# Rotary swap by bank, held-back weight splits and new instruction orders in a two-layer attention and LoRA-expert kernel on one core

## The reference

```python
x = x + attn(layernorm(x), w_qkv, w_o)            # causal, 32 query heads, 8 key heads, head size 16, rotary
x = x + ffn(layernorm(x))                         # base matmul + bias + two of eight LoRA experts, gated
x = x + attn(layernorm(x), [wq, wk, wv], wo)      # second set of attention weights
x = x + ffn(layernorm(x))                         # the same ffn weights
# x: (8, 256, 512) float32
def attn(x, w, w_o):
    q, k, v = split(x @ w)                        # 512 + 128 + 128 columns
    q, k = rope(q), rope(k)                       # pairs of neighbouring rows: (x1 c - x2 s, x1 s + x2 c)
    p = softmax(mask(q k^T / 4)); return (p v) @ w_o
def ffn(x):
    g = softmax(top2(x @ gate_w.T))
    return x @ base_w.T + base_b + 2 * sum_e g_e (x @ A_e.T) @ B_e.T
```

## Time and profile before

| what | us |
|---|---|
| median of 3 runs (lowest, highest) | 797.63 (794.98, 800.29) |
| profiled execution | 798.41 |
| span of its trace, first to last instruction | 796.6 |

### The profile page before, as it was taken

How to read it: one execution, slowest core, us unless ns; L and a number is a source line. 1 busy time by engine, 2 the same in 40 slices (tenths; PEclk the granted TensorE clock), 3 DMA queues, 4 the chain that set the end, 5 groups by cost and what they waited for, 6 DMA issues and landing times.

```text
span 796.6 us, 15039 instructions
## 1 busy us (share of the span) xinstructions
PE 741.6 (93%) x4340; PEld 558.2 (70%) x4340; DVE 564.2 (71%) x2769; ACT 492.4 (62%) x1086; POOL 567.7 (71%) x671
## 2 busy tenths in 40 slices
PE   7599889999999999799999999999999999999975
PEld 6575458777777777577777787777777768664654
DVE  5766759597586869658695968778696856877423
ACT  7425556666676756656676776767666576665522
POOL 4645784969587886968689895969778497955512
PEclk9787999999999999999999999999999999999989
DMA  8442434442434444444445635253444425342010
GB/s 316 134 118 63 121 74 114 122 105 100 106 111 128 119 129 113 141 103 116 126 119 143 158 100 122 96 125 108 117 113 126 116 68 130 104 102 76 25 49 28
DMA packets 47835, 89.30 MB, mean 112 GB/s; under 512 B 15364, under 2 KB 18180, under 8 KB 47752
## 3 DMA queue, kind: packets, MB, share of 16 engines
q1 hardware_dynamic: 45448, 87.29, 40.3%
q10 hardware_dynamic: 2304, 1.05, 0.5%
HBM read 24.34 MB, written 9.44 MB: 42 GB/s over the span
## 4 chain that ended last, share of the span: by engine, by line
PE 69%; DVE 8%; DMA 7%; POOL 6%; ACT 5%; issue 4%; SPq 1%; POOLq 0%; ACTq 0%; DVEq 0%
PE T L440 10%; PE SB L424 9%; PE SA L403 5%; PE T L382 5%; PE T L383 4%; PE T L384 4%; DVE SA L949 4%; PE SA L407 4%; PE T L452 3%; PE T L453 3%; PE T L454 3%; PE T L476 3%; DMA QK<-mT 3%; PE T L477 3%; PE T L478 3%
## 5 line engine op out<-in xcount | busy, mean ns | idle before, releaser
L949 DVE CUSTOM_DVE_ANT_0 SA<-SA,mask 128x128 f32<-128x128 f32 (+1 forms) x1024 | 332.6, 385 | 62.6 <-PE SA L407 32.4
L745 ACT ACTIVATE PT<-SB 128x512 f32<-128x512 f32 x384 | 216.2, 596 | 67.0 <-PE SB L424 56.9
L1104 POOL TENSOR_SCALAR_AFFINE_SELECT PT<-PT 128x512 f32<-128x512 f32 x256 | 159.2, 634 | 95.1 <-ACT PT L745 94.6
L424 PE MATMUL SB<-QK 100*128 100x512 f32 x384 | 149.1, 427 | 11.7 <-ACT PT L745 8.1
L949 DVE DVE_READ_ACCUMULATOR2_ANT nm<- 128x1 f32 x1024 | 140.7, 137 | 0.1
L382 PE MATMUL T<-XH,WQh 128*128 128x256 f32 x384 | 113.5, 296 | 7.6 <-DVE XL L915 6.2
L403 PE MATMUL SA<-QK 96*128 96x512 f32 x256 | 105.7, 428 | 5.9 <-DVE nm L949 5.4
L383 PE MATMUL T<-XL,WQh 128*128 128x256 f32 x384 | 110.6, 288 | 0.0
L384 PE MATMUL T<-XH,WQl 128*128 128x256 f32 x384 | 110.4, 287 | 0.0
L424 PEld LDWEIGHTS SB<-QK 100*128 100x128 f32 x384 | 71.0, 192 | 40.8 <-ACT PT L745 22.1
L440 PE MATMUL T<-PT,V 128*32 128x512 f32 x768 | 92.7, 617 | 1.3 <-POOL PT L1104 1.3
(11 more groups left out here) (102 smaller groups left out, 1641.7 us busy)
## 6 DMA issues: line engine op xcount, KB each, us to landing
QK<-Rh SPq DMA_DIRECT2D x64, 256.0 KB, 4.0
QK<-R SPq DMA_DIRECT2D x64, 192.0 KB, 3.7
Qs<-Qf SPq DMA_DIRECT2D x32, 320.0 KB, 2.9
QK<-R SPq DMA_DIRECT2D x64, 128.0 KB, 3.7
ND<-sums SPq DMA_DIRECT2D x64, 128.0 KB
ND<-EF SPq DMA_DIRECT2D x32, 128.0 KB, 2.0
mid<-X SPq DMA_DIRECT2D x16, 256.0 KB, 2.7
X<-mid SPq DMA_DIRECT2D x8, 512.0 KB, 4.1
```

Source lines behind the costliest of these rows:

```text
L424: e.matmul(SB[k % 2][:, :].rearrange("p (j q) -> p j q", j=4), keys(p, 100)[:, u % 2, i // 2, :], queries(p, 100)[:, :, min(i, 1), :], sta ...
L745: e.activation(PT[:, k % RING, :], SB[k % 2][:, :], ACT.Exp, scale=0.25).then_inc(S["ex"], 1)
L949: ins = e.tensor_tensor_reduce(x, x, mask[:, 256 - n:256], 1.0, LOWEST, ALU.add, ALU.max, nm[:, p % 2, 0, 8 * a + 2 * h + q:8 * a + 2 * h ...
L1104: e.affine_select(out=blk, in_=blk, compare_op=ALU.is_ge, fill=0.0, base=0, pattern=[[0, 4], [1, 128]], channel_multiplier=-1).then_inc(S[ ...
```

## The change

- **Swap by bank.** `sw(s)` becomes `sw(s, b)`: three pairs of transfers, each after its own bank's copy, with a semaphore of its own. `rs_` and `qe` wait for that bank's alone.
- **Splits held back.** POOL's `split_low_p(k)` waits until DVE has split chunks 0 to 3, and from k = 12 on until slot 0's rotary is through (`rl0`, `rl1`, `rl2`).
- **Staging.** `Wst` grows from 1024 to 1536 floats. Chunks 17 to 20 alternate between its halves, 21 to 24 take thirds; 17 and 18 are issued in slot 5's part of the loop, the waits of `wd` change, and each chunk has a semaphore of its own.
- **Last group.** `mu(31)` and `ol(31)` run on DVE; all others stay on POOL.
- **Output product.** `oM` with k = 0, 1 waits only for the first half's `ol`.
- **Orders.** All five lists are new. In the ramp ACT makes slot 0's copies before most weight copies, and slot 1's A groups stand among its projections. Most PSUM banks are reassigned: K/V projections use T[2], PV(2s-1) T[2] and T[3], the second tile's output product T[0].

```diff
-        Wst = sb("Wst", [P, 1024], F32)
+        Wst = sb("Wst", [P, 1536], F32)
...
-        wland += [Wst[:, 0:768] for k in range(4)]
-        wland += [Wst[:, 512 * ((k + 1) % 2):512 * ((k + 1) % 2) + 512] for k in range(4)]
+        wland += [Wst[:, c:c + 768] for c in (0, 768, 0, 768)]
+        wland += [Wst[:, c:c + 512] for c in (0, 512, 1024, 0)]
...
-                w.wait_ge(S["wlp"], {17: 8, 18: 14, 19: 15, 20: 16, 21: 17, 22: 17, 23: 18, 24: 19}[k])
+                w.wait_ge(S["wlp"], {17: 8, 18: 8, 19: 14, 20: 15, 21: 16, 22: 17, 23: 17, 24: 18}[k])
...
-            def sw(s):
-                for b in range(3):
-                    w.wait_ge(S[f"qe{b}"], s + 1)
-                    w.wait_ge(S[f"ra{b}"], s)
-                e.dma_start(Qs[0:P:2, :, :], Qf[1:P:2, 0:5, :]).then_inc(S["sw"], 16)
-                e.dma_start(Qs[1:P:2, :, :], Qf[0:P:2, 0:5, :]).then_inc(S["sw"], 16)
+            def sw(s, b):
+                w.wait_ge(S[f"qe{b}"], s + 1)
+                w.wait_ge(S[f"ra{b}"], s)
+                e.dma_start(Qs[0:P:2, chunks(b), :], Qf[1:P:2, chunks(b), :]).then_inc(S[f"sw{b}"], 16)
+                e.dma_start(Qs[1:P:2, chunks(b), :], Qf[0:P:2, chunks(b), :]).then_inc(S[f"sw{b}"], 16)
...
-                w.wait_ge(S["ol"], 2 * (n // 2) + 2)
+                w.wait_ge(S["ol"], 2 * (n // 2) + 1 + k // 2)
...
             def split_low_p(k):
+                w.wait_ge(S["wlv"], 4)
+                if k >= 12:
+                    for b in range(3):
+                        w.wait_ge(S[f"rl{b}"], 1)
                 split_low(e, w, k)
```

The PE list at the places that the prediction speaks of, ramp, loop (slot s, two parts) and end:

```diff
-            qkv(1, 1, 2, T[0]); qkv(1, 1, 3, T[0]); A(0, 0); A(0, 1); vT(1, T[3], ("qe0", 1))
+            qkv(1, 0, 0, T[3], ("ve", 0)); qkv(1, 0, 1, T[3]); A(0, 0); A(0, 1); qkv(1, 0, 2, T[3])
...
-                B(8 * s + 3, 2); qkv(s + 2, 2, 0, T[0], ("al", 2 * s + 5)); B(8 * s + 4, 0)
-                qkv(s + 2, 2, 1, T[0]); qkv(s + 2, 2, 2, T[0]); M2(4 * s + 3, T[1], ("fx", 2 * s - 3))
-                B(8 * s + 4, 1); oM(2 * s - 2, 0, T[3], ("ml", 4 * s + 2)); oM(2 * s - 2, 1, T[3])
-                oM(2 * s - 2, 2, T[3]); oM(2 * s - 2, 3, T[3]); qkv(s + 2, 2, 3, T[0])
-                oM(2 * s - 1, 0, T[1], ("ml", 4 * s + 3)); oM(2 * s - 1, 1, T[1]); oM(2 * s - 1, 2, T[1])
-                oM(2 * s - 1, 3, T[1]); PV(2 * s, T[2], ("al", 2 * s + 4), T[3], ("ox", 2 * s - 2))
+                qkv(s + 2, 2, 0, T[2], ("al", 2 * s + 4)); B(8 * s + 3, 2)
+                oM(2 * s - 2, 0, T[3], ("ml", 4 * s + 2)); qkv(s + 2, 2, 1, T[2]); qkv(s + 2, 2, 2, T[2])
+                M2(4 * s + 3, T[1], ("fx", 2 * s - 3)); oM(2 * s - 2, 1, T[3]); B(8 * s + 4, 0)
+                qkv(s + 2, 2, 3, T[2]); oM(2 * s - 1, 0, T[0], ("al", 2 * s + 5)); B(8 * s + 4, 1)
+                oM(2 * s - 2, 2, T[3]); oM(2 * s - 2, 3, T[3]); oM(2 * s - 1, 1, T[0]); oM(2 * s - 1, 2, T[0])
+                oM(2 * s - 1, 3, T[0]); PV(2 * s, T[2], ("qe2", s + 2), T[3], ("ox", 2 * s - 2))
...
-            PV(31, T[3], ("fl", 28), T[0], ("fl", 29)); fB(29, 0, T[1], ("fg", 28)); fB(29, 1, T[1])
-            fB(29, 2, T[1]); fB(29, 3, T[1]); fA(29, 0, T[0], ("oe1", 31)); fA(29, 1, T[0]); fA(29, 2, T[0])
-            fA(29, 3, T[0]); fW(14, T[3], ("oe0", 31)); fC(28, T[2]); fC(29, T[1]); oM(30, 0, T[0], ("fg", 29))
+            fA(29, 0, T[2], ("fl", 28)); fA(29, 1, T[2]); fA(29, 2, T[2]); fA(29, 3, T[2])
+            PV(31, T[3], ("fg", 28), T[1], ("fl", 29)); fB(29, 0, T[2], ("fg", 29)); fB(29, 1, T[2])
+            fB(29, 2, T[2]); fB(29, 3, T[2]); fW(14, T[1], ("oe1", 31)); oM(30, 0, T[3], ("oe0", 31))
+            oM(30, 1, T[3]); fC(28, T[0]); fC(29, T[2]); oM(31, 0, T[1], ("ll", 14)); oM(31, 1, T[1])
```

## The result

Before 798.48 us (median of 13 runs, 792.53 to 803.37), after 806.11 us (13 runs, 799.01 to 809.17): ratio 1.0091, 95% interval 1.006 to 1.0122. The kernel is 0.9% slower, where I had said 2% faster. The profiled execution of after took 808.4 us, with a span of 806.6. (Ratios are formed without runs in which the chip was in its slower state, medians over all runs, so the two can differ by a few tenths of a per cent.)

A forecast was written before the change was run, and what follows sets the result against it. PE was taken as the bound, busy 741.6 of 796.6 us; terms 5.5 + 2.0 + 1.0 + 4.0 + 2.5 = 15.0 off 798.4 gave 783.4, stated as 782.6 us since the median was 0.8 lower. Range 771 to 794.

The forecast's parts named there:

- Ramp: Start of the kernel: held-back splits, new order and earlier swap start slot 1 and its scores sooner, 5.5 us won.
- ramp given back: Rival, chance 0.20: DVE's row maxima set the pace, PE's clock halves, 0 to 1 us of ramp won; 789 to 793 us.
- Swap by bank: Other slots: six transfers for two cost SP 2.2 us per slot, which has room; nothing new late, taken as 0.
- the other branch: Swap by bank in the other slots: if SP's queue were late, the product would be, at up to 2.2 us per slot.
- Wider staging and `oM`: Slot splitting the second layer's QKV weights: oM's finer wait wins 3.4 us, later ol costs 1.4; 2.0 us won.
- Loop order: Loop slots: fewer score pairs back to back, at most 0.6 us per slot, slot 8 +1.2 once; net 1.0 us won.
- Slots 12 to 15: Late slots: more groups ahead of fW(10) win 2.0 us of wait, 1.7 of clock, 0.3 of short waits; 4 us.
- The end: Last stretch: gating wait goes, ol(31) ends 0.8 us sooner, 12 matmuls behind it instead of 24; 2.5 us won.
- Slower: Rival, chance 0.08: settled loop gets a new wait at ACT's copy; slower from 1.9 us per slot, 807 at 3.
- settled slots over 45 us: Sign of being wrong, in the loop's profile: settled slots this long, with PE waiting for ACT's copies.

The follow-up runs named there:

- g0: Changed lists up to the loop, every engine's order of the kernel before from there, without the stray matmuls of h0: ratio 0.9917 to the kernel before.
- h1: h0 with the swap by bank in the loop, six transfers back to back in place of one pair: ratio 1.0056 to the kernel before.
- h0: Changed ramp lists, loop and tail lists of before, one swap pair a slot, stray warm-up matmuls left in by the join: ratio 1.0023 to the kernel before.
- g8: Changed kernel with rr(2s-2) issued ahead of the store st(4s+2,0) in SP's loop list: 795.1 us, ratio 0.9958 to the kernel before.
- g13: g3 with chunks 21 to 24 at their old place, mu(31) and ol(31) on DVE, banks T[0] and T[1] exchanged in the tail: ratio 0.9858.
- g3: Changed ramp and PE, ACT, DVE loop lists; SP and POOL loop lists and tail of before, six swap transfers back to back: ratio 0.9943.
- g14: g0 with the store st(4s+2,2) put behind rd, so three stores stand between rd and rr: 796.17 us, ratio 0.9966 to the kernel before.
- g16: g13 with the copy oe(2s-2,0) ahead of the exponential ex(8s-4,2) on ACT in the loop: 789.3 us, ratio 0.991 to the kernel before.
- g4: Changed kernel with SP's and POOL's loop lists of before: 789.3 us, ratio 0.9863 to the kernel before.
- g5: Changed kernel with SP's loop list of before, six swap transfers back to back: 799.8 us, ratio 1.0011 to the kernel before.
- g6: Changed kernel with POOL's loop list of before: 793.0 us, ratio 0.9924 to the kernel before.
- g15: Changed kernel with the copy oe(2s-2,0) ahead of the exponential ex(8s-4,2) on ACT in the loop: ratio 1.0061 to the kernel before.

## Why the prediction was wrong, step by step

- **Ramp, -5.5: right in size, in part by luck.** -6.3 at PV(8), and -7.1 to -7.8 from PV(22) on in g0. But it did not come by the path that I had summed. Rows of after, from DVE, ACT, PE and POOL, that answer to the earlier trace rows:

```profile
14.70 0.95 DVE L152 TENSOR_TENSOR WQl<-PT,WQh 128x768 fp32r<-128x768 f32 x1
...
27.11 0.63 ACT L698 ACTIVATE R<-R 128x512 fp32r<-128x512 f32 x1 [3.55 <-DVE R L212]
...
28.82 1.11 PE L382 MATMUL T<-iden,xn 128*128 128x128 f32 x4 [5.72 <-ACT xn L790]
33.20 0.58 PE L402 MATMUL T<-XH,WQh 128*128 128x256 f32 x1 [3.26 <-DVE XL L934]
...
40.90 0.74 PE L427 MATMUL SA<-QK 96*128 96x256 f32 x4 [1.04 <-DMA QK<-R]
...
46.72 1.29 POOL L194 TENSOR_TENSOR R<-Qf,trig 128x512 f32<-128x512 f32 x1 [4.76 <-DMA QK<-R]
```

  The split is back at 0.95 as said, but slot 1's first projection starts at 33.20, not 30.7: the transposes ahead of it waited 5.7 us for ACT's normalised tile, and ACT had that tile's work behind a rotary split for which it stood 3.55 us, until 27.11. My list of DVE alone didn't see this, so of the 2.6 us that it gave 0.1 came. The scores did start 3.7 us sooner (40.90 against 44.58), and the rest grew over the next groups (PV(1) 2.7, PV(2) 5.2, PV(3) 8.3 us sooner). The rival "ramp given back" is refuted by g0.
- **Swap by bank, 0: right for the number of transfers (h1 against h0), wrong for what came with it.** The step that failed is "The waits on the copies are the old ones, now spread, so nothing new is late". I counted SP's issues (27 of 0.56 us) against the slot and found room. I did not read the order of `st` and `rr` in the new list, though the earlier trace rows show the product waiting for `ND<-sums`. What the runs showed in its place: `rr` issued behind a third store, 2.27 us instead of 1.27, the product 2.15 us later in its slot (18.04 against 15.89), and 5.8 us of the loop given back when that one store is put behind `rr` (g8). The sentence on the other branch, that a late queue makes the product late at up to 2.2 us a slot, has this size by luck, since its 2.2 were the four extra issues, and these cost nothing in h1. The Trainium skill, DMA: Bandwidth & Descriptors, on queues, rings and completion order, says that each DMA engine takes the descriptors of one queue in ring order. That a transfer meets the stores issued ahead of it would fit this, but no run shows the ring; what the rows show is the issue of `rr` alone, 2.27 us behind three stores and 1.29 behind two.
- **Wider staging and `oM`, -2.0: the term of `oM` right, the other too small.** The slot from PV(10) took 52.7 us, before 52.4. Row of after, on PE, that answers to the second of the earlier trace rows:

```profile
338.66 0.50 PE L472 MATMUL T<-WOh,OH 128*128 128x512 f32 x1 [0.33 <-POOL OL L238]
```

  From it to PV(12) are 4.3 us, where before it was 8.0: 3.7 gained, against 3.4 in the sum. But it stands 48.5 us behind PV(10), before 44.4: the second `ol` is 4.1 us late, not 1.4. I had summed POOL's work up to it, but not its waits. In the old orders the slot came out at 51.1 us in g0 and 50.8 in g13, one trace each, so the same staging and `oM` may give something there.
- **Loop order, -1.0: wrong sign, +13.0 for the loop as a whole.** The B pairs and the rest of PE's, ACT's and DVE's lists gain more than I said (3.9 us in seven slots, g3 against g0). This term put nothing for SP's and POOL's lists, and they lose 5 to 6 and 12 to 13 us by the ratios. That is the largest miss of the sum, and for POOL's part its cause stays open. My sign of being wrong, "settled slots over 45 us", came true; the wait that I named for it did not (PE at ACT's copies), it was A at `st`.
- **Slots 12 to 15, -4: wrong, +3.1 between PV(22) and PV(30).** The wait behind PV(23) is gone, but PV(22) to PV(24) took 52.7 us (before 44.5), and PV(26) to PV(28) 42.4 in place of 49.6. This is no accident of one trace: in all ten kernels with the changed tail (joins with a fault, h and g3, left aside) these two stretches took 47.4 to 55.5 and 41.7 to 42.4 us, in the kernel before and g0, g13, g14 and g16, with the old one, 44.0 to 45.1 and 48.3 to 50.0. The new lists moved work (286 matmuls from PV(22) to PV(24), before 271), and PE idled 5.8 us there, before 0.6. From PV(22) to PV(30) the ten took 164.2 to 173.7 us (g8 166.6), the other five 165.2 to 168.5 (before 167.2): no gain, where I had put 4. What lengthens PV(22) to PV(24) was not tried.
- **The end, -2.5: +1.0.** Rows of PE and DVE, from the last stretch of after, which starts at 763.89:

```profile
769.49 0.38 PE L507 MATMUL T<-iden,glo 128*128 128x128 f32 x2
...
779.99 0.79 PE L472 MATMUL T<-WOh,OH 128*128 128x512 f32 x1 [5.96 <-DVE OL L238]
...
777.86 0.69 DVE L230 TENSOR_TENSOR ND<-ND 128x512 f32<-128x512 f32 x1 [4.47 <-DMA ND<-sums]
```

  The 4.73 us wait for gating is gone, as said, and the multiply takes 0.69 instead of 1.27. But the multiply stood 4.47 us for the sums, so `ol(31)` ends 16.0 us behind PV(31), before 15.8, and not 0.8 sooner. PE now waits 5.96 us in one piece for it. Behind that wait, from 779.99 on, the mean granted clock is 0.76; before, it was 0.98 from 772 on, and over the whole stretch it fell from 0.92 to 0.83. The term had half clock for the 12 matmuls right behind the wait and no more. The eight other kernels with this tail and these steps on DVE took 41.2 to 43.0 us for the stretch, so the +1.0 is within the spread; the gain is what is missing.
- **Chances.** "Slower" had 0.08, with a new wait in every slot of the loop, from 1.9 us a slot. That is what happened, in another place; that it came to 1.9 us a slot too is chance. I gave it little since I had looked for it on ACT and PE alone. A change that rewrites five lists has more places for a new wait than I searched.

**Shown and not shown.** Shown: the place of the loss (the loop), that POOL's and SP's lists cost it, and that one exchange on SP gives back 11 us by the medians, 5.8 of them in the loop. Shown by rows, not by an edit: the circle through DVE's reciprocal; no run moved the reciprocal ahead of the maxima. Open: which entries of POOL's list make up its 12 us, beyond the 1.67 us wait for the swapped keys, why g14 loses in its first slots only, how the exchange of g8 does with POOL's list of before, and how much of the tail's spread is the order.

## What to carry to other kernels

When an order is rewritten, follow the chain on which an engine already waits, here sums out, reciprocal, sums back, product, through every queue of the new lists, the queue that only issues transfers first; a count of its issues against the slot shows nothing. Where a late step seems to delay its own cause in the next round, try one link at a time: here the exchange on SP gave 5.8 us of the loop back, and the ones on ACT and at POOL's mask nothing. To find the guilty list, join halves of the old and new lists, and compare the starts of the same groups, not the totals: in h0 these showed 9 us gained up to the stray matmuls, in a kernel whose total showed none.

## What I had not expected of the hardware

The time that SP needs to issue a transfer depends on what it has just issued. In the loop's slots the pair `rr` took 1.25 to 1.6 us where a pause or only two stores stood before it (before, g0, g4, g5, g8), and 1.9 to 2.3 right behind three (the changed kernel, g6, g14, g15; once 1.26 in g14, with a weight load between the three); the last two stores of a slot took 2.95 us together behind two others, and 1.21 in before. After the swap was split, the 128 KB parts landed in 2.3 us and the 64 KB part in 3.3, the 320 KB whole in 2.9. From the page of after (KB each, us to landing):

```profile
Qs<-Qf SPq DMA_DIRECT2D x64, 128.0 KB, 2.3
...
Qs<-Qf SPq DMA_DIRECT2D x32, 64.0 KB, 3.3
```

The Trainium skill, DMA: Bandwidth & Descriptors, on the anatomy of one DMA, gives a fixed and a variable cost, fitted on transfers issued by GpSimd. It had let me estimate 0.4 us less for the 128 KB parts, and it was 0.6. (I had read the 320 KB of the earlier trace rows as the pair's; each of its two transfers has them. Nothing in the sum hung on it.) But the smallest transfer was the slowest. It is the first of the three and is issued into the middle of the stores. Where all six are issued back to back behind the stores (h1, g3, g4, g5), the 64 KB part landed in 2.6 to 2.8 us and the 128 KB parts in 2.2 to 2.4. So part of the 3.3 us goes with its place in the queue; in none of these was it the fastest.
